# Gated attention and a mixture of experts on one core: PSUM scratch for the later blocks' choice steps, re-placed weight conversions, more filler matmuls, register loads inside block 7

## The reference

```python
query = einsum('bnc,dc->bnd', ctx, Wq) + bq;  key = einsum('bnc,dc->bnd', ctx, Wk) + bk
attention = softmax(einsum('bnd,bmd->bnm', query, key))
x = x + tanh(g_xattn) * einsum('bln,bmn->blm', layernorm(x), attention)
h = layernorm(x)
probs = softmax(gelu(h @ rw1) @ rw2)            # 8 experts
wgt, idx = top_k(probs, 2)
for e in range(8):
    Ye = gelu(h @ w1[e] + b1[e]) @ w2[e] + b2[e]   # 256 -> 1024 -> 256
    Ce = gelu(b1[e]) @ w2[e] + b2[e]
    for k in range(2):
        mask = idx[..., k] == e
        out += any(mask) * wgt[..., k:k+1] * where(mask[..., None], Ye, Ce)
x = x + tanh(g_ffn) * out
```

## Time and profile before

| | |
|---|---|
| time, median of 3 runs | 200.49 us (199.53 to 202.08) |
| profiled execution, its own time | 201.76 us |
| its span, first to last instruction | 199.9 us, mean granted TensorE clock 0.939 |
| busy: TensorE, its weight loads | 161.8 us (81%), 137.8 us (69%) |
| busy: VectorE | 133.5 us (67%) |
| busy: GpSimd | 115.6 us (58%) |
| busy: ScalarE | 102.4 us (51%) |
| DMA | 40.69 MB, mean 204 GB/s |
| chain that ended last, by engine | TensorE 45%, GpSimd 17%, VectorE 13%, DMA 11%, issue 7% |

### The profile page before, as it was taken

One profiled execution on the slowest core, in us unless ns is written; L12 is line 12 of the kernel. 1 busy time (PEld: TensorE's weight loads), 2 busy tenths in 40 slices (PEclk: granted clock), 3 DMA queues, 4 the chain that ended last, 5 costly groups with the idle time before them and its releaser, 6 DMA issues.

```text
span 199.9 us, 5212 instructions
## 1 busy us (share of the span) xinstructions
PE 161.8 (81%) x1722; PEld 137.8 (69%) x1723; DVE 133.5 (67%) x294; ACT 102.4 (51%) x256; POOL 115.6 (58%) x173
## 2 busy tenths in 40 slices
PE   6899995948169999599498599699499999998930
PEld 2457983814059999499397599598499999886610
DVE  2666589788635779989996266945566677464185
ACT  0588977727828999469487144243044433440000
POOL 0029999999868999678886414454155444203100
PEclk9999999996967999889999999999999999999955
DMA  6899354598377655945509435556166666430495
GB/s 178 252 387 331 123 152 169 181 279 271 118 211 256 232 175 201 320 147 177 197 21 387 139 113 225 216 228 234 46 241 249 247 232 219 192 113 33 125 325 200
DMA packets 21028, 40.69 MB, mean 204 GB/s; under 512 B 2741, under 2 KB 12047, under 8 KB 21010
## 3 DMA queue, kind: packets, MB, share of 16 engines
q1 hardware_dynamic: 17680, 34.54, 49.6%
q0 software_dynamic: 1872, 4.73, 7.4%
q10 hardware_dynamic: 1458, 1.19, 1.8%
HBM read 23.66 MB, written 4.60 MB: 141 GB/s over the span
## 4 chain that ended last, share of the span: by engine, by line
PE 45%; POOL 17%; DVE 13%; DMA 11%; issue 7%; SPq 3%; DVEq 1%; ACT 1%; POOLq 0%; ACTq 0%
POOL w_lo L401 11%; PE bank L1299 8%; PE bank L1301 7%; PE bank L1300 7%; PE bank L1310 7%; PE bank L1312 7%; PE bank L1311 7%; DMA stage<-in_L_ffn_w 4%; POOL w_hi L408 3%; DMA stage<-y_table 3%; DVE lnT L952 2%; DMA x_table<-probT 2%; DMA probT<-x_table,gidx 2%; DVE en L923 2%; DMA y_table<-lnx,ycol 1%
## 5 line engine op out<-in xcount | busy, mean ns | idle before, releaser
L654 ACT ACTIVATE bank<-bank,b1T 128x128 f32<-128x128 f32 x152 | 42.3, 342 | 57.7 <-PE bank L1301 57.7
L1310 PE MATMUL bank<-w_hi,cf 128*128 (+1 forms) x152 | 41.8, 275 | 9.8 <-DVE lnT L952 9.8
L401 POOL TENSOR_TENSOR w_lo<-stage,w_hi 128x256 bf16<-128x256 f32 x64 | 48.2, 787 | 0.7
L1311 PE MATMUL bank<-w_lo,cf 128*128 (+1 forms) x152 | 41.8, 275 | 0.8 <-issue 0.8
L1312 PE MATMUL bank<-w_hi,lnT 128*128 (+1 forms) x152 | 41.9, 276 | 0.0
L1300 PE MATMUL bank<-cfT,stage 128*128 128x128 bf16 x176 | 34.0, 219 | 0.0
L1299 PE MATMUL bank<-cfT,stage 128*128 128x128 f16 x176 | 34.0, 219 | 0.0
L1301 PE MATMUL bank<-cfT,stage 128*128 128x128 f16 x176 | 34.0, 219 | 0.0
L418 POOL TENSOR_TENSOR held<-cst 128x1 f32<-128x1 f32 x31 | 6.8, 218 | 39.0 <-DVE lnx L965 37.7
L952 DVE TENSOR_TENSOR lnT<-bank,cf 128x512 bf16<-128x512 f32 x38 | 26.1, 688 | 4.0 <-ACT cf L661 3.3
L519 ACT ACTIVATE w_hi<-stage 128x1024 f16<-128x1024 f32 x24 | 25.0, 1049 | 7.1 <-POOL cfT L414 5.6
(11 more groups left out here) (195 smaller groups left out, 340.7 us busy)
## 6 DMA issues: line engine op xcount, KB each, us to landing
stage<-in_L_ffn_w SPq DMA_DIRECT2D x32, 512.0 KB, 4.6
stage<-w_hi SPq DMA_DIRECT2D x12, 512.0 KB, 3.0
stage<-w_lo SPq DMA_DIRECT2D x12, 512.0 KB, 3.7
stage<-y_table SPq DMA_DIRECT2D x8, 256.0 KB, 4.7
xs<-in_x SPq DMA_DIRECT2D x2, 512.0 KB, 7.9
out<-stage SPq DMA_DIRECT2D x4, 256.0 KB, 2.7
cf<-in_ctx SPq DMA_DIRECT2D x1, 512.0 KB, 5.4
x_table<-cfT ACTq DMA_DIRECT2D x2, 256.0 KB, 4.2
```

Source lines behind the costliest of these rows:

```text
L401: last = nc.gpsimd.tensor_tensor(out=w_lo[:, q, n:n + PIECE], in0=stage[:, q % RING, n:n + PIECE], in1=w_hi[:, q, n:n + PIECE], op=ALU.sub ...
L654: last = nc.scalar.activation(h, h, ACT.Gelu, bias=bias)
L1310: mm(o, h_hi[:, u, c, :], w2_hi[:, ex, 1, c, :], start=(c == 0), stop=False)
L1311: mm(o, h_hi[:, u, c, :], w2_lo[:, ex, 1, c, :], start=False, stop=False)
```

## The change

1. **Scratch in PSUM.** The steps of `rest_of_starts`, `rest_of_blocks`, `rest_of_indices`, `experts_of_blocks`, `used_counts` and `scatter_rows` keep their intermediate values in the unused half of PSUM bank 2 or 3 (`aside[u]`; `same` in bank 5, and `scratch` in bank 6 for the first call of `scatter_rows`). A copy at the beginning of four of them brings the small input there. The step that adds `eend` goes; its constant is taken off in the comparison and in the counts. The steps now stand before the conversions `behind[i]`.
2. **Conversions.** Quarter 9's high half goes from GpSimd to ScalarE and quarter 20's from ScalarE to GpSimd. Low halves of 18 and 25 go from GpSimd to VectorE, that of 20 from VectorE to GpSimd. ScalarE does the tokens' high halves earlier, and quarters 8 and 9 after them; GpSimd does the four `token_low` right after quarter 5 and then quarters 8, 9 and 10 before the first gather. VectorE does quarters 11 and 12 after the first indices, 12 behind the first `xT_copy`. The load that waits for the first gather is 16 instead of 17. `put(3, 1)` stands before the gather for block 8.
3. **Fillers.** 4 and 4 more in the router; 12 instead of 6, 8 instead of 4 and 14 instead of 9 around the choice.
4. **Register loads.** TensorE's loads from `eb` and `used_i` stand in block 7 behind `down` at `c` = 1, 3 and 5.

```diff
+        aside = [bank[2 + u][:, 2 * P:4 * P] for u in range(2)]
-        DVE_QUARTERS = (6, 7, 11, 12, 13, 15, 17, 19, 20, 22, 23, 26, 28, 29, 30, 31)
-        POOL_HIGHS = (0, 1, 2, 3, 4, 5, 9, 27)
+        DVE_QUARTERS = (6, 7, 11, 12, 13, 15, 17, 18, 19, 22, 23, 25, 26, 28, 29, 30, 31)
+        POOL_HIGHS = (0, 1, 2, 3, 4, 5, 20, 27)
...
-                if q == 17:
+                if q == 16:
                     sp.wait_ge(gathered[0], 16)
...
             own(0, 6)
-            lows(8, 9)
-            token_low(0)
-            own(9, 10)
-            token_low(1)
-            token_low(2)
-            token_low(3)
-            lows(10, 11)
+            for b in range(4):
+                token_low(b)
+            lows(8, 11)
             wait(index_ready, 1)
...
             put(0, 0)
             refill(7, 1, 3, 16)
-            lows(18, 19)
+            own(20, 21)
             put(1, 1)
             lows(21, 22)
             put(2, 0)
             lows(24, 25)
+            put(3, 1)
             wait(index_ready, 2)
             refill(NS, 0, 4, 32)
-            put(3, 1)
-            lows(25, 26)
             own(27, 28)
             put(4, 0)
             refill(NS + 1, 1, 5, 32)
...
             high(7, 8)
+            token_high(0)
+            xnT_copy(1)
             second_deviation(2)
-            xnT_copy(1)
-            high(8, 9)
+            token_high(1)
             second_deviation(3)
             router_gelu(0)
             router_gelu(1)
-            token_high(0)
             xnT_copy(3)
-            token_high(1)
+            token_high(2)
             router_gelu(2)
-            token_high(2)
+            token_high(3)
             router_gelu(3)
-            token_high(3)
+            high(8, 9)
             send(0)
+            high(9, 10)
+            send(1)
             high(10, 11)
-            send(1)
+            send(2)
+            send(3)
             high(11, 12)
-            send(2)
-            high(12, 13)
-            send(3)
...
-            high(13, 17)
+            high(12, 16)
...
+            later = [q for q in range(16, QUARTERS) if q not in POOL_HIGHS]
...
-                    q = 17 + 2 * i + half
-                    if q >= 27:
-                        q += 1
-                    high(q, min(q + 1, QUARTERS))
+                    if 2 * i + half < len(later):
+                        high(later[2 * i + half], later[2 * i + half] + 1)
...
-            def rest_of_blocks():
+            def rest_of_blocks(spare):
+                starts = spare[:, 0:N_EXP]
+                rslot, blk_i = [spare[:, TOPK * T * n:TOPK * T * (n + 1)].bitcast(I32) for n in (1, 2)]
+                slotb = spare[:, TE:2 * TE].rearrange("p (t e) -> p t e", t=T)
+                rprod = spare[:, 2 * TE:4 * TE].rearrange("p (k t e) -> p k t e", k=TOPK, t=T)
+                same = bank[5][:, D:D + TOPK * T * REST].rearrange("p (k n) -> p k n", n=REST)
                 rank_te = rank_s[:, :].rearrange("p (t e) -> p t e", t=T)
-                step(nc.vector.tensor_tensor(out=slotb, in0=rank_te, in1=e_bc(st_[:, :]), op=ALU.add))
+                step(nc.vector.tensor_copy(starts, st_[:, :]))
+                step(nc.vector.tensor_tensor(out=slotb, in0=rank_te, in1=e_bc(starts), op=ALU.add))
...
-                step(nc.vector.tensor_tensor(out=oh_rest, in0=iota_b[:, N_EXP:BLOCKS].unsqueeze(1).broadcast_to(kb),
+                step(nc.vector.tensor_tensor(out=same, in0=iota_b[:, N_EXP:BLOCKS].unsqueeze(1).broadcast_to(kb),
                                              in1=blk_i.unsqueeze(2).broadcast_to(kb), op=ALU.is_equal))
-                nc.vector.tensor_tensor(out=oh_rest, in0=oh_rest,
+                nc.vector.tensor_tensor(out=oh_rest, in0=same,
...
-            def experts_of_blocks():
-                step(nc.vector.scalar_tensor_tensor(out=en[:, :], in0=more[:, 0:N_EXP], scalar=float(P), in1=st_[:, :],
-                                                    op0=ALU.mult, op1=ALU.add))
-                step(nc.vector.tensor_tensor(out=en[:, :], in0=en[:, :], in1=eend, op=ALU.add))
+            def experts_of_blocks(spare):
+                ends = spare[:, 0:N_EXP]
+                found = spare[:, 2 * N_EXP:2 * N_EXP + BLOCKS]
                 be = [P, BLOCKS, N_EXP]
-                step(nc.vector.tensor_tensor(out=ebge, in0=iota_b.unsqueeze(2).broadcast_to(be),
-                                             in1=en[:, :].unsqueeze(1).broadcast_to(be), op=ALU.is_ge))
-                step(nc.vector.tensor_reduce(out=ebf[:, :], in_=ebge, axis=X, op=ALU.add))
-                nc.vector.tensor_scalar(eb[:, :], ebf[:, :], float(N_EXP - 1), None, ALU.min).then_inc(eb_ready, 1)
+                behind_end = spare[:, TE:TE + BLOCKS * N_EXP].rearrange("p (b e) -> p b e", b=BLOCKS)
+                step(nc.vector.tensor_copy(ends, en[:, :]))
+                step(nc.vector.scalar_tensor_tensor(out=behind_end, in0=iota_b.unsqueeze(2).broadcast_to(be),
+                                                    scalar=float(P), in1=ends.unsqueeze(1).broadcast_to(be),
+                                                    op0=ALU.subtract, op1=ALU.is_ge))
+                step(nc.vector.tensor_reduce(out=found, in_=behind_end, axis=X, op=ALU.add))
+                nc.vector.tensor_scalar(eb[:, :], found, float(N_EXP - 1), None, ALU.min).then_inc(eb_ready, 1)
...
-            low(11)
-            low(12)
-            scatter_rows(0, N_EXP)
+            scatter_rows(0, N_EXP, first, scratch[:, 0:N_EXP])
             counts_of_choices()
             dve.wait_ge(tr_w, 2)
             nc.vector.tensor_copy(b1T[:, :], bank[7][:, 0:HC * N_EXP])
+            low(11)
             xT_copy(0, 0)
+            low(12)
+            xT_copy(1, 1)
             low(13)
-            xT_copy(1, 1)
             hidden_low(0, 0, 0)
-            ahead = {0: (15,), 1: (19,), 2: (20,), 3: (22,), 4: (23,), 5: (26,), 6: (30,)}
-            behind = {0: (17,), 5: (28, 29), 6: (31,)}
+            ahead = {0: (15,), 1: (18,), 2: (19,), 3: (22,), 4: (25,), 5: (26,), 6: (30,)}
+            behind = {0: (17,), 3: (23,), 5: (28, 29), 6: (31,)}
...
                         down(i - 1, 1 - u, i - 1, c)
+                        if i == NS - 1 and c == 1:
+                            pe.wait_ge(eb_ready, 1)
+                            pe.reg_mov(experts[0], NS - 1)
+                            pe.load(experts[1], eb[0:1, 2 * JS:2 * JS + 1])
+                        elif i == NS - 1 and c == 3:
+                            pe.wait_ge(used_ready, 1)
+                            jl = last_pair(pe)
+                        elif i == NS - 1 and c == 5:
+                            used = used_blocks(pe)
...
-            pe.wait_ge(eb_ready, 1)
-            pe.reg_mov(experts[0], NS - 1)
-            pe.load(experts[1], eb[0:1, 2 * JS:2 * JS + 1])
-            pe.wait_ge(used_ready, 1)
-            jl, used = last_pair(pe), used_blocks(pe)
             wait_weights(pe, QUARTERS - 1)
```

More of the change, by code:

```diff
@@ L145, in flamingo_moe_kernel @@
         rank_s = sb("rank_s", [P, T * N_EXP], F32)
-        more = sb("more", [P, N_EXP + 1], F32)
         st_ = sb("st_", [P, N_EXP], F32)
@@ L708, in _ @@
             nc.vector.memset(cb[:, :], 1.0).then_inc(zero_ready, 1)
-            nc.vector.memset(more[:, N_EXP:N_EXP + 1], 1.0)
             nc.vector.memset(ones16[:, :], 1.0)
@@ L892, in counts_of_choices, with rest_of_starts @@
                                         axis=X, op=ALU.add).then_inc(yidx_ready, 1)
-            def rest_of_starts():
-                step(nc.vector.tensor_tensor(out=ge, in0=nexp[:, :].unsqueeze(2).broadcast_to(ee),
+            def rest_of_starts(spare):
+                many = spare[:, 0:N_EXP]
+                more = spare[:, N_EXP:2 * N_EXP + 1]
+                ge = spare[:, TE:2 * TE].rearrange("p (a b) -> p a b", a=N_EXP)
+                ltc = spare[:, 2 * TE:2 * TE + N_EXP * (N_EXP + 1)].rearrange("p (a b) -> p a b", a=N_EXP)
+                nc.vector.memset(more[:, N_EXP:N_EXP + 1], 1.0)
+                step(nc.vector.tensor_copy(many, nexp[:, :]))
+                step(nc.vector.tensor_tensor(out=ge, in0=many.unsqueeze(2).broadcast_to(ee),
@@ new lines, in used_counts @@
+            def used_counts(spare):
+                ends = spare[:, 0:N_EXP]
+                used_f = spare[:, N_EXP:N_EXP + 3]
+                whole = spare[:, 2 * N_EXP:2 * N_EXP + 3].bitcast(I32)
+                used = ((0, P + LEAST_LAST * 2 * P, 2 * P), (1, LEAST_ODD * 2 * P, 2 * P), (2, LEAST * P, P))
+                for n, least, size in used:
+                    last = nc.vector.tensor_scalar(used_f[:, n:n + 1], ends[:, N_EXP - 1:N_EXP], float(least - P), None,
+                                                   ALU.subtract)
+                step(last)
+                step(nc.vector.tensor_copy(whole, used_f))
+                for n, least, size in used:
```

(5 more changed lines are left out.)

65 lines of the change are left out of this document (22 added, 43 removed).

## The result

| | before | after |
|---|---|---|
| time, median of 4 runs | 200.92 us (199.53 to 202.08) | 192.69 us (191.57 to 194.78) |
| profiled execution | 201.76 us, span 199.9 | 194.78 us, span 192.9 |
| mean granted clock of that execution | 0.939 | 0.960 |

The ratio is 0.9575 (95% interval 0.9485 to 0.9665), 8.2 us less. The forecast was 187.5 us with a range of 184.3 to 193.5: the right side and within the range, and 5.2 us too low. One kernel's executions differ by several us with the granted clock, and a ratio in this document compares only the executions that lie within 1.5% of the fastest of their kernel (for the order of conversions these are 2 of 11), so that it is not the quotient of the medians that stand beside it.

The account below looks back on a forecast made before the run. Bounds: the way to the first gather, TensorE and ScalarE in static blocks with VectorE and register-load stalls, then 88 us unchanged. 6.8 + 3.0 + 1.2 + 2.6 - 0.4 = 13.2 us saved; forecast 187.5 us, range 184.3 to 193.5.

Parts of the forecast that it names:

- Part 1: Static blocks: VectorE's small steps with scratch in PSUM stop waiting for GpSimd; TensorE's low-half waits and slow clock go; 6.8 us (4 to 6.8).
- part 5: GpSimd after the first gather: gather for block 9 issued about 94.5, landing about when block 8 begins; 0.4 us lost (0 to 1.5).
- Part 2: Before the first gather: reordered conversions free GpSimd at 49.3 instead of 52.3 us; gain 3.0 us (1.5 to 3.8).
- Part 3: Router, choice and block 0: added fillers and the earlier gather shorten TensorE's cold start; gain 1.2 us (0 to 2.5).
- Part 4: End of block 7: TensorE's register loads hide behind issued matmuls; 2.6 of 3.1 us gained (0.7 to 3.1).
- The rival I gave 0.04: Static blocks: VectorE's conversions, still with two SBUF inputs, starve instead, 3.3 us in two blocks; 194 us; chance 0.04.
- What follows block 8: Dynamic blocks and output, code unchanged: should again take 88 us, so no gain or loss.
- the weight stream: Weight loads before block 8: quarters issued 2.9 us apart instead of 2.2 become the bound, block 8 3.3 late; 191; chance 0.14.
- the loads and the clock giving nothing: Register loads stay exposed (+2.6) and blocks 0 and 1 still start cold (+1.2): 191.3 us; chance 0.12.

## Why the prediction was right in its direction and too low by 5 us

**Part 1, scratch in PSUM: 6.8 us forecast, 6.0 found in the stages, 2.6 to 3.7 in the time.** VectorE's timeline after the change:

```profile
71.77 0.23 DVE L899 TENSOR_TENSOR bank<-rank_s,bank 128x64 f32<-128x64 f32 x1
...
73.17 0.43 DVE L909 TENSOR_TENSOR bank<-cst,bank 128x256 f32<-128x256 f32 x1
73.64 0.42 DVE L911 TENSOR_TENSOR lnx<-bank,cst 128x256 f16<-128x256 f32 x1
...
75.31 2.60 DVE L686 TENSOR_TENSOR w_lo<-stage,w_hi 128x1024 bf16<-128x1024 f32 x1
...
78.83 0.18 DVE L866 TENSOR_SCALAR bank<-bank 128x16 f32<-128x16 f32 x1
...
84.43 0.36 DVE L921 SCALAR_TENSOR_TENSOR bank<-cst,bank 128x192 f32<-128x192 f32 x1
...
89.85 3.33 DVE L686 TENSOR_TENSOR w_lo<-stage,w_hi 128x1024 bf16<-128x1024 f32 x2
```

L909 and L911 stand for steps that took 2.18 and 0.77 us before, L866 for one of 1.95; L921 takes in the constant that the step of 3.50 added. The assumed 0.5 for 256 elements is 0.43. Blocks 4 to 6 gave 3.24 + 2.71 = 5.95 us against 6.8, with the slow clock of the earlier trace rows gone. The Trainium skill's larger overhead for PSUM ("Perfetto Trace Analysis", Optimizing Scalar/DVE Operations) does not show: reductions of 64 elements within PSUM take 0.23 in the kernel after, and the one in SBUF took 0.22 in the kernel before. That the time shows less of it has its reason below, at part 5.

**Part 2, the first gather: 3.0 forecast, 4.7 measured, some 2.8 of it by the change.** Timeline of GpSimd after the change:

```profile
48.61 1.12 POOL L419 DMA_INDIRECT probT<-x_table,gidx  x1 [0.45 <-DVE gidx L856]
...
88.32 5.39 POOL L391 TENSOR_TENSOR w_lo<-stage,w_hi 128x256 bf16<-128x256 f32 x4
...
96.08 1.01 POOL L419 DMA_INDIRECT probT<-x_table,gcol  x1
```

The gather was issued at 48.61, right behind the indices, 4.02 us earlier (the upper bound given was 3.8), and its tokens were used 2.98 us later instead of 3.64. The forecast for GpSimd's work was right: the token halves and three conversions behind quarter 5 were to take 12.1 + 1.9 = 14.0 us, and they took 14.0, from 34.15 to 48.16 (the three conversions 7.58 undisturbed, the rest of it in the token halves). But they began 1.15 us before the 35.3 that I had read from the trace before, and that is no work of the change. In the traces with the scratch in PSUM alone and with the register loads alone, whose code up to there is the old one, the first transposes began at 54.41 and 54.34 and not at 56.27. Against them the change is worth 2.8 us, and the other 1.9 are luck of the profiled execution.

**Part 3, fillers and the cold start: 1.2 forecast, 0.4 measured** between blocks 0 and 1. The clock was 1.00 in block 0, as hoped. (Block 1 had nothing to gain: it took 5.53 us in the kernel before as well, and only block 0 was slow there.) But tokens for block 2 came late (1.82 us). Its gather is the third of six in a row on GpSimd; it was issued at 52.00 and its tokens were used at 57.85, 5.8 us later, beside four weight loads issued from 51.61 to 56.36. How much of this is the queue and how much the loads was not separated. The runs without the added fillers (fillers undone; the order of conversions alone) had the clock at 1.00 in block 0 too, and no wait over 0.66 us before it: what kept the clock up was the early gather, not the fillers.

**Part 4, the register loads: 2.6 forecast, under 1 in the changed kernel.** The loads hid, even better than assumed:

```profile
L1334 PEldq TENSOR_LOAD <-eb x1: 498/498/498, 94.1 to 94.1; - x1
...
L269 PEldq TENSOR_LOAD <-used_i x2: 317/466/614, 95.1 to 96.5; - x2
```

They take 0.50, 0.32 and 0.61 us there, against 0.92 to 1.15 in the earlier trace rows. The step that failed is the one after it: what is late next.

**Part 5, GpSimd behind the gather: 0.4 forecast, 3.2 measured** (0.99 + 2.18). This is the term that was mis-sized. I had counted the instructions and placed the gather for block 9 at 94.5, with 3 to 3.5 us for landing. It was issued at 96.08, and took 5.30 in the chain. Copies of block 8's weights (issued at 94.70 and 95.37) were on their way as well, which I take for the reason; no run separates it:

```profile
96.08 5.30 DMA probT<-x_table,gcol
```

Quarter 27's four pieces, 5.39 instead of 2.56 us, were late by more. The rival I gave 0.04 held the cause: VectorE's conversions, still with both inputs in SBUF, now took a median of 1.51 us instead of 1.22, and up to 2.60. GpSimd's last four conversions before block 8 took 3.43, 3.61, 4.49 and 5.39 us, where in the kernel before the last five took 3.55, 2.74, 2.57, 2.56 and 2.75. With three quarters of GpSimd's pieces left out, VectorE's median is 1.21, and the waits are gone. That shows that GpSimd's conversions lengthen VectorE's, and that the two engines together bound blocks 5 to 8. That GpSimd's lateness comes from the contention, and not from its amount of work, is read from these lengths and not shown by a run. The runs that moved single items on GpSimd turned its wait into one for a conversion, for VectorE's low half, or for the copied weights: 195.03, 194.25 and 193.04 us, none clearly better than 192.69 to 193.49. My forecast for block 8, 97.5 to 99, was for a kernel in which the conversions cost each other nothing more than before; the run with VectorE's at 1.21, and with less work for GpSimd besides, has it at 95.77.

**What follows block 8: 0 forecast, 3.8 us lost in the profiled execution.** Two slow stretches of the clock cost 1.57 and 1.54; 0.8 in the output stage was not looked into. The first stands behind the new wait of 2.18 us. In the run with the fillers undone the wait was 2.13 and the clock in block 8 stayed at 2.4 GHz (5.56 us), and in the kernel before and in that with the fillers alone it stayed so behind 3.09 and 3.06 us of issue (5.61 us); behind waits of 2.24, 2.70 and 2.89 us in the changed kernel again, with the register loads undone and with the scratch in PSUM alone, it fell (0.76, 0.79, 0.79). So such a wait may or may not cost the clock, and its length does not decide it. What makes the difference stays open; I had no term for it. The 88 us that I expected from block 8 on are the smallest value of all the traces (88.4 to 91.1 in the runs of one part alone, 91.5 and 92.0 in the two of the changed kernel), so part of this loss is the luck of the profiled execution of the kernel before.

**The sum by stages:** 4.68 + 0.38 - 0.01 + 5.95 - 0.26 (loads, less the new waits) - 3.77 = 6.97 us, the difference of the spans. It is 6.2 less than the 13.2 of the forecast: 3.8 behind block 8, 2.5 at the loads and GpSimd (2.2 forecast), 0.9 in part 1 and 0.8 in part 3, less the 1.7 that the first gather gave beyond its term. The medians differ by 8.2; the profiled execution of the kernel after, 194.78, lies 2.1 above its median, that of before 0.8 above its own.

**The range and the rivals.** The likeliest rival, the weight stream, did not come: the last quarter was issued at 84.8 us, where the forecast needed 83.5 and the rival 93.8. The upper end of the range, 193.5, was set by it and by the loads and the clock giving nothing; the time lies within it for other reasons, GpSimd beside VectorE and the clock behind block 8. In that the range was lucky.

## What to carry to other kernels

When a stall is taken away, look up which queue is next at that point and count it as carefully as the stall itself: here the same lateness of one weight quarter appeared as a wait for a gather, for a conversion, or for a copy, depending on the order, and only less work for GpSimd took it away. Small steps of VectorE beside a busy GpSimd belong in PSUM, at least one input of them; their length in SBUF ranged from 0.17 to 3.50 us for 8 elements. That the parts measured alone add up to the whole (8.4 or 11.0 us, by ratios or by medians, against 8.2) proves little when each is known to 1 to 3 us; the waits in each trace showed that more than one part was cut short by the same neighbour. And a stage that one execution ran well, the first gather or the clock behind block 8, should be looked up in a second trace of the same code before it is counted as gained or lost.

## What was not expected of the hardware

- Two engines' subtractions from SBUF stretch each other: VectorE's 1.22 us conversions went to 2.60, and four GpSimd pieces from 2.56 to 5.39.
- A gather that shares its time with two weight copies took 5.30 us from issue to use, where the median to landing is 3.2 in the same trace and 2.8 in the one before.
- A register load of TensorE took 0.30 to 1.15 us, with no change of the instruction.
- The first gather's tokens came 1.4 to 2.0 us later than in the other traces with the same code up to there, in the one trace in which a 512 KB load was issued beside it.
- Behind idle times of 2.1 to 3.1 us of TensorE block 8 took 5.6 us in some traces and 6.9 to 7.2 in others, and the longest of these idle times were among those that cost nothing.
